# Sixteen experts' outputs added up in two sums instead of one, in a fused kernel for deformable attention, a recurrence and a mixture of experts

## What is computed

```python
h = tok(x)                                  # 1024 queries a batch, 8 sampled points each, softmax over the points
h = concatenate([h, txt], axis=1)           # 16 x 1152 x 64
h = h + recurrence(layernorm(h))            # complex diagonal recurrence over the 16 batches
h = h + ffn(layernorm(h))

def ffn(x, gate_w, gate_b, w1, w2, w3):     # 16 experts, hidden size 128, all computed for every token
    probs = softmax(x @ gate_w + gate_b)
    top_probs, top_idx = top_k(probs, 2)
    dispatch = sum(one_hot(top_idx, 16) * normalised top_probs)          # two of 16 are not zero
    hidden = silu(x @ w1[e]) * (x @ w2[e])  # per expert e
    expert_out = hidden @ w3[e]
    return sum over e of expert_out[e] * dispatch[e]
```

## Time and profile before

| | before |
|---|---|
| median of 3 runs | 2246.7 us (2244.17 to 2251.53) |
| the profiled execution, its own time | 2242.19 us |
| its span in the profile | 2240.4 us |
| TensorE busy (matmuls) | 2017.2 us, 90% |
| TensorE weight loads | 1837.6 us, 82% |
| VectorE busy | 1996.7 us, 89% |
| ScalarE, GpSimd busy | 942.2 us (42%), 1454.0 us (65%) |
| TensorE's granted clock, mean | 0.954 |
| VectorE's fused operations of line 975 | 2304, of 276 ns each |

### The profile page before, as it was taken

How to read it: one execution, slowest core, us unless ns; L and a number is a source line. 1 busy time by engine, 2 the same in 40 slices (tenths; PEclk the granted TensorE clock), 3 DMA queues, 4 the chain that set the end, 5 groups by cost and what they waited for, 6 DMA issues and landing times.

```text
span 2240.4 us, 45957 instructions
## 1 busy us (share of the span) xinstructions
PE 2017.2 (90%) x15249; PEld 1837.6 (82%) x15249; DVE 1996.7 (89%) x6209; ACT 942.2 (42%) x2040; POOL 1454.0 (65%) x1657
## 2 busy tenths in 40 slices
PE   2468999989898999999899998989999998999899
PEld 1356789889798988889798897989888898988788
DVE  1257899999999999999999999999999999999998
ACT  1224443444444444444444444444444444433333
POOL 0388767578585858758575775858587685858700
PEclk9779999999999999999999999999999999998999
DMA  8787536466564646666463665746376674532200
GB/s 200 214 238 207 172 106 179 139 186 194 162 189 112 182 123 193 188 169 194 111 183 111 189 191 165 198 114 188 104 197 183 169 199 120 175 88 85 68 3 6
DMA packets 363145, 346.80 MB, mean 155 GB/s; under 512 B 49312, under 2 KB 313632, under 8 KB 362784
## 3 DMA queue, kind: packets, MB, share of 16 engines
q1 hardware_dynamic: 313760, 209.59, 34.8%
q0 software_dynamic: 49152, 134.28, 20.1%
HBM read 205.89 MB, written 137.89 MB: 153 GB/s over the span
## 4 chain that ended last, share of the span: by engine, by line
PE 60%; DVE 27%; issue 8%; POOL 2%; DMA 1%; ACT 1%; DVEq 0%; POOLq 0%; ACTq 0%
PE bank_o L637 15%; PE bank_h L628 10%; PE bank_h L629 9%; PE bank_d L693 9%; PE bank_d L703 7%; DVE ob L975 5%; DVE hid L964 4%; DVE wsam L1053 2%; DVE v_sb L1088 2%; PE bank_a L715 2%; PE bank_p L658 2%; POOL gath L574 2%; DVE v_sb L1081 2%; PE bank_p L657 1%; PE bank_p L663 1%
## 5 line engine op out<-in xcount | busy, mean ns | idle before, releaser
L574 POOL DMA_INDIRECT gath<-table,idx x1024 | 1127.0, 1101 | 271.4 <-issue 237.5
L637 PEld LDWEIGHTS bank_o<-w_sb,hid 128*128 128x128 f32 x4608 | 636.2, 199 | 75.4 <-issue 60.6
L637 PE MATMUL bank_o<-w_sb,hid 128*128 128x64 f32 x4608 | 630.8, 275 | 43.7 <-DVE ob L975 42.6
L628 PE MATMUL bank_h<-xsplit,w 128*128 128x384 f32 x1536 | 616.4, 401 | 28.3 <-DVE hid L964 27.7
L787 ACT ACTIVATE silu<-bank_h 128x384 f32<-128x384 f32 x768 | 380.6, 496 | 481.5 <-PE bank_h L629 476.5
L629 PE MATMUL bank_h<-xsplit,w 128*128 128x384 f32 x1536 | 532.0, 346 | 0.0
L975 DVE SCALAR_TENSOR_TENSOR ob<-bank_o,disp,ob 128x64 f32<-128x64 f32 x2160 | 474.5, 276 | 3.7 <-PE bank_o L637 3.4
L964 DVE TENSOR_TENSOR hid<-silu,bank_h 128x384 f32<-128x384 f32 x768 | 420.6, 548 | 25.1 <-ACT silu L787 18.2
L628 PEld LDWEIGHTS bank_h<-xsplit,w 128*128 128x128 f32 x1536 | 301.2, 196 | 59.4 <-DVE hid L964 35.2
L1053 DVE TENSOR_TENSOR wsam<-gath,cw 128x1024 f32<-128x1024 f32 x256 | 312.3, 1220 | 25.8 <-DMA gath<-table,idx 19.6
L693 PE MATMUL bank_d<-eye,wsam 128*128 128x128 f32 x2048 | 281.8, 283 | 30.1 <-DVE wsam L1053 26.6
(11 more groups left out here) (142 smaller groups left out, 1864.4 us busy)
## 6 DMA issues: line engine op xcount, KB each, us to landing
table<-pixmaj SPq DMA_DIRECT2D x80, 1024.0 KB, 10.0
xin<-x_dram SPq DMA_DIRECT2D x256, 256.0 KB
table<-pixmaj SPq DMA_DIRECT2D x32, 960.0 KB
table<-pixmaj SPq DMA_DIRECT2D x16, 1088.0 KB
gath<-table,idx POOLq DMA_INDIRECT x1024
out_dram<-ob SPq DMA_DIRECT2D x48, 96.0 KB
gath<-w_dram SPq DMA_DIRECT2D x4, 512.0 KB, 9.3
interp_sb<-interp_dram SPq DMA_DIRECT2D x1, 1024.0 KB, 5.5
```

The costliest lines, as they stand in the source:

```text
L574: pool.indirect_dma_start(out=gath[buf][:, p, :, :].rearrange("p a c -> p (a c)"), out_offset=None, in_=table[par], in_offset=bass.Indirec ...
L628: mm(bank[:, 0:GC], w12[:, e, which, 0, :], xsplit[gp][:], start=True, stop=False)
L637: last = mm(bank_o[n % 2][:, C * k:C * (k + 1)], hid[:, n % HB, 128 * k:128 * (k + 1)], w3_sb[:, e, :], start=True, stop=True)
```

## The change

Experts of even number are summed in `ob` as before, those of odd number in a new pair of tiles `odd`. Expert 1 starts the odd sum, by a product without a third operand (`tensor_scalar`). None of the 48 operations of a group waits for another one of VectorE any more. A new piece M2 on VectorE adds `odd` to `ob`, 128 x 192, once for each group; the store of the group waits for it (`ob_done`).

```diff
+    ("M2", "dve"): [(i,) for i in range(3)],
...
+        odd = [sb(f"odd{i}", [128, GT, C]) for i in range(2)]
...
+        ob_done = sem("ob_done")
...
             def out_group(b, g, gp):
-                wait(sp, eo_added, GT * NE * (NGRP * b + g + 1))
+                wait(sp, ob_done, NGRP * b + g + 1)
...
                         for k in range(GT):
-                            if e:
-                                dve.wait_ge(eo_added, GT * (n - 1) + k + 1)
-                            stt(ob[gp][:, k, :], bank_o[n % 2][:, C * k:C * (k + 1)], disp[gp][:, k, e:e + 1],
-                                (ob[gp] if e else h2[g])[:, k, :], ALU.mult, ALU.add).then_inc(eo_added, 1)
+                            eo = bank_o[n % 2][:, C * k:C * (k + 1)]
+                            share = disp[gp][:, k, e:e + 1]
+                            if e == 1:
+                                ins = ts(odd[gp][:, k, :], eo, share, None, ALU.mult)
+                            elif e % 2:
+                                ins = stt(odd[gp][:, k, :], eo, share, odd[gp][:, k, :], ALU.mult, ALU.add)
+                            else:
+                                ins = stt(ob[gp][:, k, :], eo, share, (ob[gp] if e else h2[g])[:, k, :], ALU.mult, ALU.add)
+                            ins.then_inc(eo_added, 1)
+                    elif kind == "M2":
+                        g = args[0]
+                        gp = gpar(par, g)
+                        dve.wait_ge(eo_added, GT * NE * (NGRP * b + g + 1))
+                        tt(ob[gp][:], ob[gp][:], odd[gp][:], ALU.add).then_inc(ob_done, 1)
```

The table `ORDER` is new for all engines. On VectorE each of the 48 groups gets one letter q; apart from that the strings are the old ones but for pieces that change places with a neighbour, most of them in the first two batches, a few in each later one. A line of VectorE's string, from the middle of the run:

```diff
-        "nHkGHwGkHGHyGHzGHmkGrHmknGHeGHsGtHGmkHGfmHnkGHhGHuGvHjmGHxmGnHBGHwGHHCGyGDHzGHGrHkGHGHksGtHGHGHkmGHm",
+        "mGHDxmGnHkGHwGkHGHyGHzGHmkGrHmknGHeGHsGtHqGmkHGfmHnkGHhGHuGvHjmGHxmGnHBGHwGHHCGyGDHzGHGrHkGHGHksGtHq",
```

More of the change, by code:

```diff
@@ L173 @@
[L173 to L176 removed]
+        "aaaaaaaaaaaaaaaabbbbbbbbcdehiaaaaaaaallmmlaaalammllmamalaabbbbbbbblcmdmellmmlhialsamtmualaaalwmyGmaG",
@@ new lines @@
+        "lGFaGFGFGlFGmFGmFGlFGFGFaFGaalamGmlFstGluFmGFmGlwFaFyGFGalamamGFGFlsbbGtFGFlGFmuGmFGFbblGbFbbGFblcmw",
+        "dmeGFlGFyGlFGmFGmFGFlGFGFlmGFsmGtFGlFGuFlGhFimGFmGFaaaGFwGaFGFyaFGaaGFaGFGFGFlGFGFlsGFtmGFmGFulGFGlF",
+        "aGFmGFmwGFlGFylGFGmFaGmFaGFlGFalaGFmGFsmGtFaGlFaGFluGFamGFbmbGFbbGbFbbwbGcFdlGFylGFGmFGmFGFlGeFlGFmG",
+        "FsmGtFGlFGuFlGhFmiGFmGFaaaGFwGaFGFyaFGaaGFaGFGFGFlGFGFlsGFtmGFmGFulGFGlFaGFmGFmwGFlGFylGFGmFaGmFaGFl",
+        "GFalaGFmGFsmGtFaGlFaGFluGFamGFbmbGFbbGbFbbwbGcFlGFyGlFGmFGmFdGFlGeFlGFmGFsmGtFGlFGuFlGhFimGFmGFaaaGF",
@@ new lines @@
+        "wGaFGFyaFGaaGFaGFGFGFlGFGFlsGFtmGFmGFulGFGlFamGFGFmwGFlGFyGlFGmFaGmFaGFlGaFalGFmGFsmGtFaGlFaGFluGFam",
+        "GFbmbGFbbGbFbbbwGcFdlGFyGlFGmFGmFGFlGeFlGFmGFsmGtFGlFGuFlGhFimGFmGFaaaGFwGaFGFyaFGaaGFaGFGFGFlGFGFls",
+        "GFtmGFmGFulGFGlFaGFmGFmwGFlGFyGlFGmFaGmFaGFlGFalaGFmGFsmGtFaGlFaGFluGFamGFbmbGFbbGbFbwbbGcFlGFyGlFGm",
+        "FGmFdGFlGeFlGFmGFsmGtFGlFGuFlGhFimGFmGFaaGFwaGFaGFyFGaaGFaGaFGFGFlGFGFlsGFtmGFmGFulGFGlFaGFmGFmwGFlG",
+        "FylGFGmFaGmFaGFlGFalaGFmGFsmGtFaGlFaGFluGFamGFbmbGFbbGbFbwbbGFclGFyGlFGmFGmFdGFlGeFlGFmGFsmGtFGlFGuF",
@@ new lines @@
+        "lGhFimGFmGFaaaGFwGaFGFyaFGaaGFaGFGFGFlGFGFlsGFtmGFmGFulGFGlFaGFmGFmwGFlGFylGFGmFaGmFaGFlGFalaGFmGFsm",
+        "GtFaGlFaGFluGFamGFbmbGFbbGbFbbwbGcFlGFyGlFGmFGmFdGFlGeFlGFmGFsmGtFGlFGuFlGhFimGFmGFaaGFwaGFaGFyFGaaG",
+        "FaGaFGFGFlGFGFlsGFtmGFmGFulGFGlFaGFmGFmwGFlGFyGlFGmFaGmFaGFlGFalaGFmGFsmGtFaGlFaGFluGFamGFbmbGFbbGbF",
+        "bbwbGcFdlGFyGlFGmFGmFGFlGeFlGFmGFsmGtFGlFGuFlGhFimGFmGFaaaGFwGaFGFyaFGaaGFaGFGFGFlGFGFlsGFtmGFmGFulG",
+        "FGlFamGFGFmwGFlGFylGFGmFaGmFaGFlGFalaGFmGFsmGtFaGlFaGFluGFamGFbmbGFbbGbFbbwbGcFlGFyGlFGmFGmFdGFlGeFl",
@@ new lines @@
+        "stGlmGmGwaGyGalamamGGsGtGlGmGmGGBGblcmwdmGGGlyGmGmGGGlmGsmGtGgGlGhmGmGaaaGwGaBGaGaaGyaGGGGGlsGtmGmGG",
+        "GlaGmGmwGGlGyGmaGmaGGalaGmGsmGtaGBaGlGamGmGGwbGcdGlGyGmGmGGlGmGsmGtGgGlGhmGmGaaaGwGaBGaGaaGyaGGGGGls",
+        "GtmGmGGGlaGmGmwGGlGyGmaGmaGGalaGmGsmGtaGBaGlGamGmGGwbGcGGlGymGmdGGlGmGsmGtGgGlGhmGmGaaaGwGaBGaGaaGya",
+        "GGGGGlsGtmGmGGGlamGGmwGGGlyGmaGmaGGaalGmGsmGtaGBaGlGamGmGGbwGcdGGlyGmGmGGlGmGsmGtGgGlGhmGmGaaaGwGaBG",
+        "aGaaGyaGGGGGlsGtmGmGGGlaGmGmwGGGlyGmaGmaGGalaGmGsmGtaGBaGlGamGmGGwbGcGGlGymGmdGGlGmGsmGtGgGlGhmGmGaa",
```

120 lines of the change are left out of this document (50 added, 70 removed).

## The result

| | before | changed |
|---|---|---|
| median of the runs, us | 2248.1 (4 runs) | 2268.5 (4 runs, 2260.1 to 2269.9) |
| ratio | | 1.0083, 95% interval 1.0053 to 1.0114 |
| profiled execution, own time / span, us | 2242.19 / 2240.4 | 2260.11 / 2258.3 |
| mean granted clock of TensorE | 0.954 | 0.948 (the other three runs 0.944 to 0.947) |

The changed kernel is slower by 20 us, 0.8%. The forecast was 2251.1 us, and the range ended at 2263: the result lies outside. The profiled execution is the fastest of the four, so its trace shows a little less than the median does.

What follows compares the result with a forecast made beforehand. TensorE and VectorE were taken to share the bound, changing hands within each batch. Only joining additions counted, 0.5 + 3.5 + 0.4 = 4.4 us, on a median of 2246.7: 2251.1 us, range 2242 to 2263.

Steps and rivals of the forecast that it cites:

- Waits removed: VectorE's fused operations: taking away 2160 waits, 45 operations in each of 48 groups, changes nothing, 0 us.
- The product: Expert 1 on VectorE: 144 products in place of fused operations, taken as 0 us, within 3.2 us either way.
- The joining addition: 48 VectorE additions of 0.27 us: first boundaries 0, second 0.5, third 3.5, the end 0.4 us.
- The new order: Apart from the q, pieces only change places with a neighbour: 0, plus or minus 2 us.
- the sum: The prediction's total for the joining additions by place: 0.5 + 3.5 + 0.4 = 4.4 us, of 13 us added.
- The clock rival: Pause at batch end: later VectorE lengthens it, seven more batches turn long at 1.7 us each, 2263.0 us; chance 0.14.
- Every addition paid: Pauses behind the first two boundaries move along and swallow nothing: 13.1 us, 2259.8 us; chance 0.2.
- its sign in the trace: Behind first boundaries the pause stays, and distances between second boundaries grow by 0.8 us.

Runs made afterwards that it cites:

- the one without the waits: The changed kernel without its 48 joining additions, stores waiting for the group's last fused operation instead: 2255.2 us, ratio to the kernel before 1.0021.
- the kernel with two heaps of times: The whole change in the work order of the kernel before, each join put in at the same count of expert sums: 2259.7 us, ratio 1.0026.

## Why the prediction was wrong

**Waits removed, 0 us: right in the instructions.** Fused operations have 276 and 277 ns, a three 0.66 us. The Trainium skill ("VectorE: DVE Perf Modes", "The DRAIN you can't avoid") says that a chain with a semaphore on each operation measured the same as one with a single semaphore, and this trace agrees: 276 ns with the waits, 276 and 277 without. One thing stays open: of two kernels in the same order, the one without the waits is 7.6 us faster (2255.2 against 2262.8), though neither their traces' distances nor their instructions differ. That it moves how often the falls are long, as in the kernel with two heaps of times, would fit; it was not shown.

**The product, 0: right.** 275 ns where the fused operation has 276. The Trainium skill ("VectorE: DVE Perf Modes", "Why PSUM operands drop a tier") has a float32 operand in PSUM at the lowest tier, and this trace agrees: the 254 ns of a source in SBUF did not carry over.

**The joining addition, 4.4 us: right as far as it went.** The step is 0.27 us. First boundaries swallow it (four of them cost 1.1 us over the whole run, and the pause shrank by 0.95). Second boundaries cost 0.2 us a batch for four where the fall lies within the pause (five batches), and 1 us in the one batch with a fall of 3.4 us. Third boundaries pay in full, 1.3 us for four. With TensorE's pause filled in both kernels the whole change costs 1.8 us by the medians. In the batches that have no fall at all the distance grows from a mean of 129.40 (6 batches) to 129.59 (10 batches), 0.19 us each or 3 us over 16, where the sum had 4.

**The new order, "0, and plus or minus 2 us": the step that failed.** Alone it costs 14.4 us. I had taken it for swaps of neighbours, which TensorE's string does not bear out, and had priced moved pieces by their instructions and their waits, as adding none. With the pause filled, the order and all the rest of the change together cost 2 to 3 us, so a direct price of the order above that would have to be given back by another part. What the traces suggest is that a piece that stands elsewhere shifts the pause at the end of the batch by tenths of a microsecond against the moment at which the clock falls. An addition does so too: alone, in the old order, it also cost 12.7 us, where the sum had 4.4.

**The clock rival, 2263.0 us, chance 0.14: the right mechanism, priced and weighted too low.** It was written that I am wrong if the mean clock falls below 0.954 with distances of 131 us in most batches. It fell to 0.948 and below, with ten of 12 distances at 130.6 or more, five of them above 131. Its price of 1.7 us for each batch that turns long knew only one thing that can get worse, the length of the fall. The second is where a fall begins: In these two kernels 6.8 us from inside the pause go with 129.1 to 129.7 us, 6.8 us from behind it with 130.6 to 131.3. Six of 12 batches had the good case before, one has it now. Eleven traces have this pause unfilled and in its old place, 132 batches in all, and in them the fall that comes goes with where it starts against the end of the pause (some batches have a further fall elsewhere):

| the fall begins | falls | their length, us | distances, us (median) |
|---|---|---|---|
| 1.1 to 0.4 us ahead of the pause's end | 21 | 6.8, all | 129.1 to 130.9 (129.7) |
| from 0.3 us ahead of it to 0.6 us behind | 47 | 10.2, all | 131.1 to 133.4 (131.8) |
| 0.6 to 1.9 us behind it | 47 | 6.8, all | 130.0 to 132.0 (130.9) |
| 1.95 to 2.8 us behind it | 17 | 3.4 in 15, 6.8 in 2 | 128.8 to 132.1 (130.1) |

And the rival was asked for a longer pause; the pause stayed at 2.5 us or less, and moved.

**Every addition paid, 2259.8 us, chance 0.2:** its sign in the trace came true, the pause behind first boundaries stayed at 1.28 us in most batches, and the reason given did not. It stays where the clock has been low just before, and with the clock up it shrinks to 0.99: TensorE's lateness, not VectorE's, makes it. That may also account for most of the 0.5 to 0.7 us by which batches of the same kind have grown, up to three additions of 0.27, where the sum had 0.25; this was not separated.

What stays open is the rule by which a kernel falls into one pattern or the other. The trace of the four additions behind second boundaries changes from one to the other in mid-run with no edit between. Part of it can be read in the kernel before. Its falls at 597.9, 727.6, 857.4 and 987.1 us are 129.7 us apart, while the pauses end at 599.0, 728.5, 857.9 and 987.2, some 129.4 apart. So the fall begins 1.1, 0.8, 0.6 and then 0.2 us ahead of the pause's end; at 0.2 it lasts 10.2 us, the batch takes 131.3, and the next fall begins 1.8 us behind the pause. A batch that is tenths of a microsecond longer or shorter therefore lands elsewhere in the table a few batches later. I can show where the fall begins against the pause; I could not say beforehand to which side an edit moves it. The order alone and the addition alone were not shown with the pause filled where the kernel before takes its usual time: that their costs were the clock's is argued from the distances, and shown only for the change as a whole. The join on GpSimd and the additions at third boundaries are slower without more time at 1.2 GHz: the second by its instructions, the first for a cause that stays open.

## What to carry to other kernels

Where a kernel's TensorE pauses once per round and the granted clock falls behind that pause, look first at when within the pause the fall begins and how often it is long: there tenths of a microsecond decide over 1 to 2 us a round, and a reordering that should cost nothing cost 14 us here. Such a kernel can't be used to price small edits as it stands; fill the pause with matmuls that nobody needs (here ten, in a bank whose content is dead), in both versions, and compare those. It may also be an improvement, if a small one: the kernel before with its pause filled, 2240.4 us, beats both kernels of this study. But where everything ran 10% slower, the same matmuls cost it 21 us (ratio 1.011), so time it where it is to run.

## What the runs showed of the hardware that I had not expected

- Matmuls without any use made the changed kernel 29.7 us faster and the kernel before 4.6 us. The granted clock fell from 2.4 to 1.2 GHz behind a pause of 2.49 us, and stayed at 1.00 over ten of 12 batches of the changed kernel once that pause alone was filled; shorter ones, of 0.5 to 1.2 us, remained. In the kernel before with the pause filled, three of 12 batches still had a fall at this place.
- The falls at this place last 3.4 us (15), 6.8 (70) or 10.2 (47), nothing between, in the 132 batches read; the same pause of 2.48 to 2.49 us was followed by each of the three. Which one it is goes with where the fall begins: from 0.3 us ahead of the pause's end to 0.6 behind it, always 10.2 us.
- One kernel, on one chip, took times from 2240.5 to 2251.5 us and from 2258.2 to 2265.2 us, with none between, in 12 executions; the kernel before fills that gap in 35.
- `tensor_scalar` with its source in PSUM takes 275 ns for 128 x 64, from SBUF 254.
- In the kernel that joins on GpSimd, a VectorE operation of line 1004 on 128 x 192 took 462 ns on average; in the one without a join, 352.
